# In units 17 to 30, VectorE sums the next unit's weight quarters behind the sum of two banks

## The chip, the core and the metric

The kernel runs on one core of a Trainium2 chip. The metric is the time of one launch on the device, in microseconds (us), as a median of several runs. A core has TensorE for matrix products (PE in the profile, PEld for its loading of weights), VectorE (DVE), ScalarE (ACT) and GpSimd (POOL) for work element by element, and SyncE (SP), whose queue here only starts transfers (DMA). Each engine takes its instructions in the order in which they are written and waits at semaphores for the others. TensorE writes into eight banks of 128 x 512 float32 numbers.

## What is computed

One transformer block of 2048 tokens and 512 features: a recurrent attention block on its first step, with a feed-forward half, and then a gated feed-forward block. The third stage, of which this case is, computes half of the last lines:

```
x = x + _L0_attn_ref(_layernorm(x), ...)
# _L0_ffn_ref, on h_shard = _layernorm(x):
gate_up = jnp.einsum('bsh,oh->bso', h_shard, w_gate_up)   # w_gate_up: 4096 x 512
gate, up = jnp.split(gate_up, 2, axis=-1)
h = jax.nn.silu(gate) * up
out = jnp.einsum('bsi,hi->bsh', h, w_down)
```

## The kernel before

**Three passes.** Every float32 product is made as three passes over numbers that are split in a high part (rounded by ScalarE) and a low part (what the rounding left, a subtraction on GpSimd or VectorE): high x high, high x low, low x high, summed in a bank.

**Units.** Both feed-forward parts are cut in 48 units. Units 0 to 15 (`is_key`) are the first part, two stages of eight; units 16 to 31 are the third stage, units 32 to 47 the fourth (`FIRST = (0, 8, 16, 32)`). A unit of the third stage takes 128 rows of gate and 128 of up against two blocks of 512 tokens. It does these four blocks of products with seven, in the manner of Strassen and Winograd: the four weight quarters and four sums of them (S1 to S4) meet seven combinations of the tokens (`combo`), which were made at the stage's start. The products land in four banks: X, Y, V and Z.

**TensorE's order in a unit** (`unit(u)` on TensorE) is: X product (p1), V product (p7), output tile, Y product (p6), X again (p2), output tile, Y (p5), output tile, Z (p4), Y (p3), output tile. A product is six matmuls, and so is an output tile, which multiplies the inner rows of an earlier unit with the matrix of the second layer. Unit 17 has two output tiles instead of four, behind p5 and p3.

**What VectorE does in a unit** (`unit(u)` on VectorE): it adds an output tile's bank to its rows (`accumulate`, L1664), makes Z from Y and the seventh product (`seed`, L1754), waits for p5, and makes V from the same two (`sum_v`, L1758), which the Y product p3 waits for, since it goes on in bank Y. Then it multiplies the Silu of X and of Y with Z and V (`gate`, L1768). Between these stand the sums of the next unit's weights (`sums(u + 1)`, L1603, L1604, L1606, L1608): from four quarters of 128 x 256 numbers it makes S1 to S4 in the tile `quart`.

**The weights' way.** SyncE loads the quarters of a unit into `quart` (`load_quart`, L510) when the unit before has no more use for it, that is when its low parts are done. ScalarE rounds the quarters (`unit_left_hi` part 0, L1113) and, when the sums are there, the four sums (part 1, L1116). GpSimd makes the low parts (`unit_left_lo`, L2072), two instructions for each part. TensorE's X product wants part 0, and its V product part 1. SyncE then keeps the whole in memory for the fourth stage (`keep_left`, L514).

**ScalarE's order in a unit**: copy of X (L1266), copy of V (L1272), rounding of the inner rows of the unit before (L1149), L1113, L1116, then the Silu of X (L1173), the rounding of the second layer's rows (L1126), and the Silu of Y (L1173). The X product of the next unit waits for the first Silu, its V product for both gates.

**GpSimd's order in a unit**: the low parts of the inner rows (L2112), L2072 twice for part 0, L2072 twice for part 1, the low part of the second layer's rows (L2107), and in some units two steps of the norm of a block (L2090, L2092).

**The norm of the second half of the tokens** runs beside the third stage. SyncE moves each of two blocks in 32 x 32 squares (`move_norm3`, L545, eight transfers behind `keep_left` of units 22 and 23 and of 27 and 28), stores rows of means and scales (L554), and loads them back broadcast (`load_rows`, L563). GpSimd (L2090, L2092) and for the last block VectorE too (L1720, L1722, at the end of units 28 and 29) wait for these rows. SyncE's queue is in order as well: `load_tall`, `load_quart`, `keep_left`, the moves and rows, unit by unit. `load_tall` (L525) brings rows of the second layer, L532 and L533 bring what the first part's end needs.

The order is written out by hand on every engine; nothing is scheduled by a program.

Of the kernel before, what the change touches and what calls it, by code (L numbers as in the profile page):

```python
# [78 lines left out]
FIRST = (0, KEY_UNITS, KEYS, KEYS + GATE_UNITS)  # L79
# [14 lines left out]
def made_place(stage, c):  # L94

    return (MADE_LATER if stage else MADE_FIRST).index(c)


def stage_of(u):
    return max(n for n in range(STAGE_COUNT) if FIRST[n] <= u)  # L100


def stage_start(u):
    return u in FIRST


def is_key(u):
    return u < KEYS
# [29 lines left out]
def tiles_in(u, slot):  # L138

    first, last = (tiles_until(u - 1), tiles_until(u)) if u else (0, 0)  # L140
    if u == KEYS + 1:
        return (first + slot - 2,) if slot >= 2 else ()
    if last == TILES:
        return tuple(range(first + slot, min(first + slot + 1, last)))
    share = (last - first) // 4
    return tuple(range(first + share * slot, first + share * (slot + 1)))
# [65 lines left out]
FRESH = tuple(u for u in range(UNITS) if stage_of(u) % 2 == 0)  # L212
# [6 lines left out]
def fresh_until(u):  # L219

    return len([f for f in FRESH if f < u])
# [34 lines left out]
def build(nc, x, x_feat, wts, wide, tall, down, vectors, identity, out):  # L256
# [3 lines left out]
    with ExitStack() as ctx:  # L260
# [1127 lines left out]
        def _(dve):  # L1388
# [210 lines left out]
            def sums(u):  # L1599

                done = 4 * fresh_until(u)
                dve.wait_ge(quart_loaded, 16 * (fresh_until(u) + 1))
                dve.tensor_tensor(quart[:, 4, :], quart[:, 0, :], quart[:, 3, :], ALU.add).then_inc(sums_done, 1)  # L1603
                dve.tensor_tensor(quart[:, 6, :], quart[:, 1, :], quart[:, 0, :], ALU.subtract).then_inc(sums_done, 1)  # L1604
                dve.wait_ge(sums_done, done + 1)
                dve.tensor_tensor(quart[:, 5, :], quart[:, 4, :], quart[:, 1, :], ALU.subtract).then_inc(sums_done, 1)  # L1606
                dve.wait_ge(sums_done, done + 3)
                dve.tensor_tensor(quart[:, 7, :], quart[:, 2, :], quart[:, 5, :], ALU.subtract).then_inc(sums_done, 1)  # L1608
# [20 lines left out]
            def first_chunk_right_lo():  # L1629
                for i in range(2):  # L1630
                    dve.wait_ge(right_hi, i + 1)
                    dve.tensor_tensor(right[:, 0, i, 1, :], tall_staged[i][:], right[:, 0, i, 0, :].bitcast(F32),
                                      ALU.subtract).then_inc(first_right_lo, 1)

            def combo_lo_of(stage, c):
                for k in range(2):
                    dve.wait_ge(combo_hi, 2 * (SEVEN * stage + made_place(stage, c)) + k + 1)
                    dve.tensor_tensor(combo[:, c, k, 1, :], combined(stage, c, k), combo[:, c, k, 0, :].bitcast(F32),  # L1638
                                      ALU.subtract).then_inc(combo_lo, 1)

            def make_t2(stage, tiles=range(2)):
                dve.wait_ge(combo_lo, 2 * (SEVEN * stage + made_place(stage, B11) + 1))
                dve.wait_ge(t_made, 8 * stage + 4)
                for k in tiles:
                    dve.tensor_tensor(combined(stage, T2, k), combined(stage, B22, k), combined(stage, T1, k),
                                      ALU.subtract).then_inc(t_made, 1)
# [8 lines left out]
            def accumulate(n):  # L1655
                h, s = divmod(n, SUBS)
                b = block_of_half(h)
                dve.wait_ge(out_psum, n + 1)
                tile = resid[:, b, s, :]
                if h // 2 in FIRST[:2]:  # L1660
                    dve.wait_ge(x1_kept[b], 16)
                    dve.tensor_copy(tile, A[s][:]).then_inc(added, 1)
                else:
                    dve.tensor_tensor(tile, A[s][:], tile, ALU.add).then_inc(added, 1)  # L1664
# [82 lines left out]
            def seed(u):  # L1747
                dve.wait_ge(p6, u + 1)
                dve.wait_ge(seventh_copied, u + 1)
                if u == 0:  # L1750
                    dve.wait_ge(sr_ready, SUBS * BLOCKS)
                elif is_key(u - 1):
                    dve.wait_ge(silu_done, silu_by(u - 1, 1))
                dve.tensor_tensor(Z[:], Y[:], seventh[:], ALU.add).then_inc(z_seeded, 1)  # L1754

            def sum_v(u):
                dve.wait_ge(p5, u + 1)
                dve.tensor_tensor(V[:], Y[:], seventh[:], ALU.add).then_inc(v_summed, 1)  # L1758
# [11 lines left out]
            def side_sum(kk, c):  # L1770

                dve.wait_ge(gated, 2 * (FIRST[3] + 2 * kk - KEYS) + (2 if c == T1 else 4))
                if c == T1:
                    if kk:
                        dve.wait_ge(side_lo, side_made(kk - 1, T2))
                    else:
                        dve.wait_ge(combo_lo, 2 * SEVEN * STAGE_COUNT)
                    dve.tensor_tensor(extra[:, 0, :], made[:, 1, :], made[:, 0, :], ALU.subtract).then_inc(side_sums, 1)
                elif c == T3:
                    dve.wait_ge(side_sums, 4 * kk + 1)  # L1780
                    dve.tensor_tensor(made[:, 1, :], made[:, 3, :], made[:, 1, :], ALU.subtract).then_inc(side_sums, 1)
                elif c == T2:
                    if kk:
                        dve.wait_ge(side_lo, side_made(kk - 1, T4))
                    dve.wait_ge(side_sums, 4 * kk + 1)
                    dve.tensor_tensor(extra[:, 1, :], made[:, 3, :], extra[:, 0, :], ALU.subtract).then_inc(side_sums, 1)
                else:
                    dve.wait_ge(side_lo, side_made(kk, B21))
                    dve.wait_ge(side_sums, 4 * kk + 3)
                    dve.tensor_tensor(made[:, 2, :], made[:, 2, :], extra[:, 1, :], ALU.subtract).then_inc(side_sums, 1)  # L1790
# [80 lines left out]
            def unit(u):  # L1871

                after = stage_of(u + 1) if u + 1 < UNITS and stage_start(u + 1) else None
                def some(slot):
                    for n in tiles_in(u, slot):
                        accumulate(n)

                if u == FIRST[3] + 1:
                    side_sum(0, T1)

                if after is not None:
                    combo_lo_of(after, B11)
                some(0)
                if after is not None:
                    make_t2(after, range(1))
                seed(u)
                if after is not None:
                    make_t2(after, range(1, 2))
                    combo_lo_of(after, T3)
                if u + 1 in FRESH and u > 1:  # L1890
                    sums(u + 1)
                if u == FIRST[2]:
                    dve.wait_ge(combo_lo, 2 * (SEVEN * 2 + made_place(2, T4) + 1))
                    combo_lo_of(2, B22)
                if stage_start(u) and u and u != FIRST[2]:
                    combo_lo_of(stage_of(u), T4)
                if is_key(u):
                    last_norm(u, 0)
                some(1)
                if u == 1:  # L1900
                    sums(u + 1)
                sum_v(u)
                if stage_start(u) and u and u != FIRST[2]:
                    combo_lo_of(stage_of(u), B22)
                if u == FIRST[3] + 1:
                    down_sums_of(0)
                if u == 0:
                    first_chunk_right_lo()
                if u in SUMS_UNIT and is_key(u):
                    right_sums(SUMS_UNIT.index(u))  # L1910
                if after is not None:
                    combo_lo_of(after, T2)
                    combo_lo_of(after, B21)
                some(2)
                if not is_key(u):
                    gate(u, 0)
                    gate(u, 1)
                if after is not None:
                    make_t4(after)
                some(3)  # L1920
                if after is not None and after != 2:
                    combo_lo_of(after, T1)
                last_norm(u, 1)
                if u in SUMS_UNIT and not is_key(u):
                    right_sums(SUMS_UNIT.index(u))
# [78 lines left out]
            for u in range(GROUP_UNIT):  # L2004
                unit(u)
# [290 lines left out]
```

## Time and profile before

| | us |
|---|---|
| median of 3 runs | 1047.43 |
| lowest and highest | 1046.34, 1048.19 |
| profiled execution | 1050.09 |
| its span, first to last instruction | 1048.3 |

The span is what the profile shows of the profiled execution, 1.8 us shorter than its time. TensorE is busy for 99% of it, VectorE 69%, GpSimd 60%, ScalarE 50%. A unit of the third stage takes 14.96 us where TensorE doesn't wait; unit 17 begins at 574.58 us and the V product of unit 31 at 788.09 us from the span's start. The times of instructions below are from that start. A matmul follows the one before it after 0.227 us, and its recorded end is modelled, so waits of TensorE are best read from the distance of starts.

### The profile page before, as it was taken

What the parts mean: (1) busy time and instruction counts of PE and PEld (TensorE: products, weight loads), DVE (VectorE), ACT (ScalarE), POOL (GpSimd) and SP (SyncE); (2) the same over time, 40 slices, a digit from 0 to 9 for tenths busy, and PEclk for the clock granted to TensorE, in tenths of its full rate; (3) what the DMA queues carried; (4) which work ended last, traced back from release to release, by engine and by line L of the source; (5) the groups of instructions that cost most, each with busy time, mean ns of one, the idle gap of its engine ahead of it and who ended that gap; (6) DMA issues with size and microseconds to landing.
All of it is one profiled execution on the core that took longest, in us unless ns stands there. A gap on an engine that the chain in (4) does not pass through costs nothing.

```text
span 1048.3 us, 13498 instructions
## 1 busy us (share of the span) xinstructions
PE 1035.7 (99%) x4616; PEld 855.3 (82%) x4616; DVE 719.6 (69%) x1227; ACT 520.4 (50%) x874; POOL 626.5 (60%) x512
## 2 busy tenths in 40 slices
PE   8999999999999999999999999989999999999999
PEld 7778888888888888888888788878878888888887
DVE  7899866786545565566569677688699566666655
ACT  6867888766444354333345433333335334444442
POOL 6796673735755555444547656579594356565652
PEclk9999999999999999999999999999999999999999
DMA  9100325277653344745634666765746445444532
GB/s 347 58 21 0 61 80 114 89 234 267 232 182 130 131 161 131 227 147 139 159 95 147 224 219 237 165 241 196 203 164 221 151 154 179 155 154 161 161 101 81
DMA packets 81123, 165.60 MB, mean 158 GB/s; under 512 B 39072, under 2 KB 39456, under 8 KB 76192
## 3 DMA queue, kind: packets, MB, share of 16 engines
q1 hardware_dynamic: 65600, 116.43, 33.5%
q0 software_dynamic: 15168, 48.24, 15.4%
q8 instruction: 37, 0.61, 0.2%
q14 instruction: 30, 0.25, 0.1%
q10 hardware_dynamic: 288, 0.09, 0.0%
HBM read 101.80 MB, written 58.74 MB: 153 GB/s over the span
## 4 chain that ended last, share of the span: by engine, by line
PE 78%; DVE 8%; POOL 5%; DMA 3%; SPq 2%; ACT 2%; issue 2%; DVEq 0%; ACTq 0%
PE bank L665 12%; PE bank L667 12%; PE bank L666 12%; PE bank L654 11%; PE bank L656 11%; PE bank L655 11%; POOL operand L2039 3%; PE bank L827 2%; PE bank L826 2%; PE bank L825 2%; SPq L545 2%; DMA quart<-wide 1%; DVE combo L1638 1%; POOL left L2072 1%; POOL weights L2027 1%
## 5 line engine op out<-in xcount | busy, mean ns | idle before, releaser
L665 PE MATMUL bank<-combo,left 128*128 128x512 f32 x672 | 262.1, 390 | 2.6 <-DVE bank L1758 2.6
L666 PE MATMUL bank<-combo,left 128*128 128x512 f32 x672 | 261.5, 389 | 0.0
L667 PE MATMUL bank<-combo,left 128*128 128x512 f32 x672 | 261.5, 389 | 0.0
L1664 DVE TENSOR_TENSOR resid<-bank,resid 128x512 f32<-128x512 f32 x176 | 119.9, 687 | 114.5 <-PE bank L656 113.6
L2112 POOL TENSOR_TENSOR inner<-made,inner 128x512 fp32r<-128x512 f32 x96 | 128.4, 1359 | 115.7 <-ACT inner L1149 115.6
L2072 POOL TENSOR_TENSOR left<-quart,left 128x512 fp32r<-128x512 f32 x96 | 115.9, 1230 | 78.1 <-ACT left L1116 39.4
L665 PEld LDWEIGHTS bank<-combo,left 128*128 128x128 f32 x672 | 126.1, 188 | 30.7 <-DVE bank L1758 4.3
L654 PE MATMUL bank<-right,inner 128*128 128x512 f32 x384 | 149.5, 389 | 1.6 <-POOL inner L2112 1.6
L656 PE MATMUL bank<-right,inner 128*128 128x512 f32 x384 | 149.4, 389 | 0.0
L655 PE MATMUL bank<-right,inner 128*128 128x512 f32 x384 | 149.4, 389 | 0.0
L666 PEld LDWEIGHTS bank<-combo,left 128*128 128x128 f32 x672 | 126.2, 188 | 26.1
L667 PEld LDWEIGHTS bank<-combo,left 128*128 128x128 f32 x672 | 126.2, 188 | 26.1
L2039 POOL TENSOR_TENSOR operand<-made,operand 128x512 fp32r<-128x512 f32 x64 | 83.3, 1354 | 32.7 <-ACT operand L993 32.7
L1158 ACT ACTIVATE made<-bank 128x512 f32<-128x512 f32 x64 | 37.6, 587 | 97.9 <-PE bank L667 97.9
L654 PEld LDWEIGHTS bank<-right,inner 128*128 128x128 f32 x384 | 72.1, 188 | 16.9 <-POOL inner L2112 2.0
L1768 DVE TENSOR_TENSOR made<-bank,made 128x512 f32<-128x512 f32 x64 | 44.1, 690 | 59.7 <-ACT made L1173 37.6
L1173 ACT ACTIVATE made<-bank 128x512 f32<-128x512 f32 x64 | 38.0, 593 | 94.4 <-PE bank L667 94.4
L655 PEld LDWEIGHTS bank<-right,inner 128*128 128x128 f32 x384 | 72.1, 188 | 15.0
L656 PEld LDWEIGHTS bank<-right,inner 128*128 128x128 f32 x384 | 72.1, 188 | 14.9
L1116 ACT ACTIVATE left<-quart 128x1024 fp32r<-128x1024 f32 x24 | 25.4, 1060 | 93.6 <-DVE quart L1608 93.6
L2107 POOL TENSOR_TENSOR right<-tall_staged,right 128x512 fp32r<-128x512 f32 x46 | 61.0, 1339 | 16.5 <-ACT right L1126 16.4
L654 PE MATMUL bank<-operand,weights 128*128 128x512 f32 x176 | 69.3, 394 | 1.1 <-DVE resid L1573 0.5
(199 smaller groups left out, 2018.1 us busy)
## 6 DMA issues: line engine op xcount, KB each, us to landing
kept_left<-left SPq DMA_DIRECT2D x24, 1792.0 KB, 8.1
left<-kept_left POOLq DMA_DIRECT2D x24, 1024.0 KB, 7.2
left<-kept_left POOLq DMA_DIRECT2D x24, 768.0 KB, 5.0
quart<-wide SPq DMA_DIRECT2D x24, 512.0 KB, 4.0
tall_staged<-tall SPq DMA_DIRECT2D x48, 256.0 KB, 5.2
raw<-kept SPq DMA_DIRECT2D x32, 256.0 KB, 5.4
landed<-wts SPq DMA_DIRECT2D x20, 256.0 KB, 6.3
resid<-x POOLq DMA_DIRECT2D x4, 1024.0 KB, 9.5
```

Source lines behind the costliest of these rows:

```text
L654: pe.matmul(acc, left(0), right(0), start=first, stop=False)
L655: pe.matmul(acc, left(0), right(1), start=False, stop=False)
L656: return pe.matmul(acc, left(1), right(0), start=False, stop=last)
L665: pe.matmul(acc[:], hi, combo[:, c, k, 0, :], start=fresh and k == 0, stop=False, skip_group_check=True)
L666: pe.matmul(acc[:], hi, combo[:, c, k, 1, :], start=False, stop=False, skip_group_check=True)
L667: mm = pe.matmul(acc[:], lo, combo[:, c, k, 0, :], start=False, stop=k == 1, skip_group_check=True)
L1664: dve.tensor_tensor(tile, A[s][:], tile, ALU.add).then_inc(added, 1)
L1768: dve.tensor_tensor(tile, (Z, V)[b][:], tile, ALU.mult).then_inc(gated, 1)
L2039: pool.tensor_tensor(place(kind, b, k, 1), made[:, (n + k) % RING, :], place(kind, b, k, 0).bitcast(F32), ALU.subtract).then_inc(op_lo, 1)
L2072: lo = pool.tensor_tensor(left[u % 2][:, 1, a[0]:a[0] + n, :], quart[:, a[0] + 1:a[0] + 1 + n, :], left[u % 2][:, 0, a[0]:a[0] + n, :].bit ...
L2107: pool.tensor_tensor(right[:, g % 2, i, 1, :], tall_staged[i][:], right[:, g % 2, i, 0, :].bitcast(F32), ALU.subtract).then_inc(right_lo, 1)
L2112: pool.tensor_tensor(inner[:, h % 4, i, 1, :], made_at(n), inner[:, h % 4, i, 0, :].bitcast(F32), ALU.subtract).then_inc(inner_lo, 1)
```

## The change

In the third stage, except for its first unit (16), `sums(u + 1)` moves from behind the seed to behind `sum_v`. That is so in 14 units, 17 to 30; unit 31 has no sums, since the fourth stage loads its weights ready made. Units of the first stage and units 15 and 16 keep their place.

```
@@ VectorE, unit(u) @@
                 if after is not None:
                     make_t2(after, range(1, 2))
                     combo_lo_of(after, T3)
-                if u + 1 in FRESH and u > 1:
+                if u + 1 in FRESH and u > 1 and u <= FIRST[2]:
                     sums(u + 1)
...
                 if u == 1:
                     sums(u + 1)
                 sum_v(u)
+                if u + 1 in FRESH and u > FIRST[2]:
+                    sums(u + 1)
                 if stage_start(u) and u and u != FIRST[2]:
                     combo_lo_of(stage_of(u), B22)
```

On VectorE, in unit 17: L1664 is the last accumulation of unit 16, L1754 the seed, L1603 to L1608 the sums (`quart`), L1758 is `sum_v`, and L1768 the two gates.

```order
 L1754 TENSOR_TENSOR bank<-bank,e_56 128x512
-L1603 TENSOR_TENSOR quart<-quart 128x256
-L1604 TENSOR_TENSOR quart<-quart 128x256
-L1606 TENSOR_TENSOR quart<-quart 128x256
-L1608 TENSOR_TENSOR quart<-quart 128x256
-L1758 TENSOR_TENSOR bank<-bank,e_56 128x512
+L1758 TENSOR_TENSOR bank<-bank,e_56 128x512
+L1603 TENSOR_TENSOR quart<-quart 128x256
+L1604 TENSOR_TENSOR quart<-quart 128x256
+L1606 TENSOR_TENSOR quart<-quart 128x256
+L1608 TENSOR_TENSOR quart<-quart 128x256
 L1664 TENSOR_TENSOR resid<-bank,resid 128x512
```

The sums are moved past `sum_v` alone. On VectorE in units 18 to 30, 24 and 29 among them, the accumulation of the output tile behind p2 (the first L1664) stands between seed and `sum_v` as well:

```order
-L1603 TENSOR_TENSOR quart<-quart 128x256
-L1604 TENSOR_TENSOR quart<-quart 128x256
-L1606 TENSOR_TENSOR quart<-quart 128x256
-L1608 TENSOR_TENSOR quart<-quart 128x256
-L1664 TENSOR_TENSOR resid<-bank,resid 128x512
-L1758 TENSOR_TENSOR bank<-bank,e_56 128x512
+L1664 TENSOR_TENSOR resid<-bank,resid 128x512
+L1758 TENSOR_TENSOR bank<-bank,e_56 128x512
+L1603 TENSOR_TENSOR quart<-quart 128x256
+L1604 TENSOR_TENSOR quart<-quart 128x256
+L1606 TENSOR_TENSOR quart<-quart 128x256
+L1608 TENSOR_TENSOR quart<-quart 128x256
```

The sums are moved past that accumulation and past `sum_v`. The other engines' orders are the same as before.

## Rows read from the trace of the kernel before

**Rows 1.** Head of the page: span, then busy time, share and count.

```profile
span 1048.3 us, 13498 instructions
...
PE 1035.7 (99%) x4616; PEld 855.3 (82%) x4616; DVE 719.6 (69%) x1227; ACT 520.4 (50%) x874; POOL 626.5 (60%) x512
```

**Rows 2.** Waits of TensorE from 500 to 830 us: total us, times, longest.

```profile
PE bank L665 <- DVE bank L1758: 2.6, 3, 1.3
```

**Rows 3.** Timeline of VectorE, unit 18: start, us, line, tiles.

```profile
593.49 0.70 DVE L1754 TENSOR_TENSOR bank<-bank,e 128x512 f32<-128x512 f32 x1 [0.67 <-PE bank L667]
594.10 0.69 DVE L1603 TENSOR_TENSOR quart<-quart 128x256 f32<-128x256 f32 x1
...
597.13 0.42 DVE L1608 TENSOR_TENSOR quart<-quart 128x256 f32<-128x256 f32 x1
...
598.08 0.69 DVE L1758 TENSOR_TENSOR bank<-bank,e 128x512 f32<-128x512 f32 x1
```

**Rows 4.** Timelines of ScalarE, GpSimd, SyncE's queue and TensorE, units 18 and 19.

```profile
597.60 1.06 ACT L1116 ACTIVATE left<-quart 128x1024 fp32r<-128x1024 f32 x1 [4.46 <-DVE quart L1608]
598.56 0.58 ACT L1173 ACTIVATE made<-bank 128x512 f32<-128x512 f32 x1
...
594.46 2.36 POOL L2072 TENSOR_TENSOR left<-quart,left 128x512 fp32r<-128x512 f32 x2
598.73 2.54 POOL L2072 TENSOR_TENSOR left<-quart,left 128x512 fp32r<-128x512 f32 x2 [1.92 <-ACT left L1116]
...
601.30 0.33 SPq L510 DMA_DIRECT2D quart<-wide  x1
...
602.81 0.39 PE L665 MATMUL bank<-combo,left 128*128 128x512 f32 x1
...
604.17 0.39 PE L665 MATMUL bank<-combo,left 128*128 128x512 f32 x1
```

**Rows 5.** Timeline of VectorE, unit 15: first and last of four sums.

```profile
551.00 0.41 DVE L1603 TENSOR_TENSOR quart<-quart 128x256 f32<-128x256 f32 x1
...
552.11 0.42 DVE L1608 TENSOR_TENSOR quart<-quart 128x256 f32<-128x256 f32 x1
```

**Rows 6.** Timelines of GpSimd and TensorE, unit 17.

```profile
581.42 2.17 POOL L2072 TENSOR_TENSOR left<-quart,left 128x512 fp32r<-128x512 f32 x2 [0.19 <-ACT left L1113]
...
582.74 0.39 PE L665 MATMUL bank<-combo,left 128*128 128x512 f32 x1
...
584.99 0.50 PE L665 MATMUL bank<-combo,left 128*128 128x512 f32 x1 [0.73 <-DVE bank L1758]
```

**Rows 7.** Timelines of SyncE's queue, VectorE, GpSimd and TensorE, units 23 and 24.

```profile
661.14 0.33 SPq L510 DMA_DIRECT2D quart<-wide  x1
...
673.67 0.38 SPq L554 DMA_DIRECT2D rows<-row_stats  x1
678.25 0.33 SPq L563 DMA_DIRECT2D extra<-rows  x1
...
690.55 1.40 DVE L1608 TENSOR_TENSOR quart<-quart 128x256 f32<-128x256 f32 x1
...
687.36 2.88 POOL L2112 TENSOR_TENSOR inner<-made,inner 128x512 fp32r<-128x512 f32 x2
...
688.85 0.50 PE L654 MATMUL bank<-right,inner 128*128 128x512 f32 x1 [1.56 <-POOL inner L2112]
...
693.21 0.50 PE L665 MATMUL bank<-combo,left 128*128 128x512 f32 x1 [1.33 <-DVE bank L1758]
```

**Rows 8.** Timelines of VectorE, GpSimd and TensorE, end of unit 28 and unit 29.

```profile
758.08 1.08 DVE L1720 TENSOR_TENSOR raw<-resid,extra 128x512 f32<-128x512 f32 x1 [1.29 <-DMA extra<-rows]
...
762.06 0.69 DVE L1754 TENSOR_TENSOR bank<-bank,e 128x512 f32<-128x512 f32 x1
...
766.15 1.40 DVE L1608 TENSOR_TENSOR quart<-quart 128x256 f32<-128x256 f32 x1
...
762.92 2.91 POOL L2112 TENSOR_TENSOR inner<-made,inner 128x512 fp32r<-128x512 f32 x2
...
768.81 0.50 PE L665 MATMUL bank<-combo,left 128*128 128x512 f32 x1 [0.51 <-DVE bank L1758]
```

More of the change, by code:

```diff
@@ L1889, in unit @@
                     combo_lo_of(after, T3)
-                if u + 1 in FRESH and u > 1:
+                if u + 1 in FRESH and u > 1 and u <= FIRST[2]:
                     sums(u + 1)
@@ L1902, in unit @@
                 sum_v(u)
+                if u + 1 in FRESH and u > FIRST[2]:
+                    sums(u + 1)
                 if stage_start(u) and u and u != FIRST[2]:
```

## The prediction

> **What bounds the kernel now.** I read the page's head first, then the waits of TensorE, then the timeline of one ordinary unit of the third stage engine by engine, and last the units in which TensorE waits. TensorE is busy for 99% of the span [rows 1], so whatever is not late for TensorE costs nothing: the question is only at which products it waits, by how much, and what will be late next. In and around the third stage it waits three times for the sum of two banks [rows 2], in units 17, 24 and 29, and once for the low part of an inner tile, in unit 24.
>
> An ordinary unit shows the frame. The X product and the V product of unit 19 start 1.36 us apart [rows 4], and every product and every output tile takes one such slot: the unit is 11 slots, 14.96 us. Counting back five slots from 602.81, the Y product that sum_v waits for (p5) starts at 596.01; counting back three more, the one that the seed waits for starts at 591.93, and the seed starts 1.56 us behind it [rows 3]. So sum_v could start at 596.01 + 1.56 = 597.57; it starts at 598.08 [rows 3]. Its result is wanted two slots before the end, at 600.09. In an ordinary unit the sums in front of it therefore cost nothing, and the change gains nothing there.
>
> **What the change moves.** In 14 units (17 to 30) the four sums go behind one accumulation and sum_v on VectorE. No instruction is added, and no DMA, wait or tile is. What queues behind the sums is the chain that makes the next unit's weights: ScalarE rounds four parts (L1116), with both Silus of the unit behind it in its queue, GpSimd makes the low parts (L2072), and SyncE then issues the load of the quarters of the unit after (L510) [rows 4].
>
> *The sums themselves, ordinary unit.* Before, they run from 594.10 to 597.55 [rows 3], 3.45 us, while GpSimd works on parts 0 to 2 from 594.46 to 596.82 [rows 4]. With GpSimd idle the four take from 551.00 to 552.53, 1.53 us [rows 5]. Behind sum_v, GpSimd is idle: its parts 0 to 2 are done at 596.82 and its next work needs the sums. I take the 1.53 us: start 597.57 + 0.60 (the spacing of sum_v's twin, the seed, and the first sum [rows 3]) = 598.17, end 599.70, against 597.55. The upper bound is the old 3.45 us, and I come back to it as a rival. In the slowed pieces a sum ends some 0.28 us behind the GpSimd instruction that runs beside it. The Trainium skill (SBUF — State Buffer, section "Who interferes with whom") says why: a VectorE instruction with two SBUF inputs and a GpSimd instruction exclude one another for a whole instruction. By that the sums take the lone time here, as rows 5 shows it; if both instead shared a rate, the old 3.45 us would stay, and the sum would be that of the third case below.
>
> *The chain behind them.* ScalarE's L1116 starts 2.15 us later, at 599.75; the Silu of X follows 0.96 us behind it [rows 4], at 600.71, and is wanted by the next X product at 602.81; GpSimd starts L2072 1.13 us behind L1116 [rows 4], at 600.88, and needs 2.54 us: 603.42. The V product wants it at 604.17 [rows 4]. So 0.7 us are left of 2.9 us, and the ordinary unit costs **0**. If that cover were gone, each us would be paid in every unit. The load of the next quarters goes out 2.15 us later too, at 603.4, but the sums that use it are later by as much, and it lands long before.
>
> *Unit 17, a gain.* The quarters land late here, ScalarE's first part (L1113) and GpSimd's parts 0 to 2 at 581.42 [rows 6] follow, the sums run beside these and sum_v behind them, and the product that wants V starts at 584.99, where the one before it began at 582.74 [rows 6]: 2.25 us instead of 1.36, so 0.89 us, and some 0.1 us that the first product behind a wait takes longer. After: p5 starts at 582.74 - 2 x 1.36 = 580.02, sum_v at 581.58, the sums at 582.2; GpSimd's parts 0 to 2 [rows 6] still overlap the first two, so they end at about 584.5, 0.2 us later than now. Then L1116 at 584.6 and L2072 until 584.6 + 1.13 + 2.54 = 588.3, while the V product of unit 18 would be free to start at 584.10 + 3 x 1.36 = 588.18. So about 0.15 of the 1.0 us comes back: **-0.86 us**.
>
> *Unit 24, a loss.* SyncE's queue holds, behind the load of quarters, the moves of the norm, the store and broadcast of its rows (L563 at 678.25) and the next load of quarters. It starts when unit 23's low parts are done, which is 2.15 - 0.86 = 1.29 us later than now, and between that load, at 661.14, and L563 it never waits for anything but its own transfers: eight moves, two loads, a store of rows and its landing. So the rows land 1.29 us later, GpSimd's norm rows and behind them the inner low parts (687.36) too, and the output tile at 688.85 that waits for them starts at 690.14 [rows 7]. From there the old wait for V goes: the product at 693.21 [rows 7] would start 1.36 us behind its predecessor, and 2 x 1.36 us or a little more behind the tile, at 692.99; 1.49 + 0.15 us are saved. The sums are again as slow as now (four of them beside GpSimd, the last at 690.55 for 1.40 us [rows 7]), 1.29 us later, so L1116 is at 693.3 and the low parts at 693.3 + 1.13 + 2.54 = 696.95, for a V product at 697.07: just in time. Net of unit 24: +2.15 - 1.64 = **+0.5 us**, to -0.35 in all.
>
> *Units 29 and 30, a loss.* The same queue, now for the fourth block: the rows land 1.95 us later than at 758.08 (2.15 and 0.15 for a GpSimd step that slides, less 0.35). VectorE itself waits for them ahead of the seed: L1720 at 760.03, the seed at 764.01 instead of 762.06 [rows 8]. The product behind it was due at 763.71, and starts at 764.75: one wait takes the place of the other, and the product that wants V starts three slots later at 768.8, as now (768.81 [rows 8]). Now sum_v runs early, at 766.3, but the sums stand at 766.9 with GpSimd's inner parts and parts 0 to 2 beside them (the first two now at 762.92 [rows 8], then at 764.9, and the next two until 769.75): they end near 770.5 instead of 766.15 + 1.40 = 767.55 [rows 8]. L1116 at 770.5, Silu of X 771.5 to 772.05, low parts 771.6 to 774.2. The next X product, due at 771.54, waits 0.5 us for the Silu, and V, due at 773.46 then, waits 0.8 us for the low parts: it starts at 774.24, where now it is at 773.03. Net of the pair: +1.21 - (-0.35) = **+1.55 us**. Unit 30's chain comes out at 789.2 for a V product due at 789.2: nothing more. Units 31 and later have no sums, and keep the shift.
>
> **Sum.** -0.86 + 0.5 + 1.55 = +1.2 us on the span of 1048.3 us [rows 1], so 1049.5; the profiled execution took 1050.09 us and the median of the runs is 1047.43, so I forecast **1048.6 us** for the median, a change of 0.1%. A measurement of this kernel tells about 0.2%, 2.1 us, from no change.
>
> **Rivals.**
>
> *Everything late falls, nothing comes back.* Then the three waits go: 1.0 + 1.6 + 0.8 = 3.4 us, and the time is 1044.0. For it: the waits are in the trace with VectorE's sum as their releaser [rows 2]. Against it: the later load and the later moves in SyncE's queue, and ScalarE's queue with the Silus behind L1116. It wants that queue to have slack, which it has not between 661 and 678 [rows 7]. 18%, with the mixed cases that gain over 2.1 us.
>
> *A late SyncE queue costs more than I reckon.* The same two places with larger sizes: the row transfers land on a DMA load that they did not meet before, or VectorE's norm row of unit 29, 1.08 us at 758.08 [rows 8], is caught behind a GpSimd instruction and takes as much longer as a sum does, 1.1 us. One us or two more at unit 30, paid by the X product through the Silu: +2.1 to +5 us, up to 1052.4. It decides from 0.9 us over my figures. 23%.
>
> *The margin of every unit is gone.* If the sums in their new place still take 3.45 us, L2072 ends at 605.3, 1.2 us behind the V product at 604.17, and in some 13 units that is +15 us: 1063. It begins to cost as soon as the four last over 1.53 + 0.7 = 2.2 us. Against it: nothing on GpSimd can run beside them. 7%.
>
> *It does nothing.* That the sums do move shows in the order of the two kernels; if waits for V are only swapped for waits on the Silu or the low parts, the time is that of before, 1047.4, inside my forecast.
>
> **How the numbers follow.** My case, within 2.1 us of before: 52%. Faster 18%, slower 23 + 7 = 30%. The range 1045.0 to 1052.2 leaves out the last rival (7%), the full form of the first (some 8%) and the edge of the second (3%).
>
> **What would show it right or wrong.** In the changed kernel's profile: ordinary units with sums of 0.41 us each and L1116 2.1 us later against sum_v's product; waits for the bank sum gone in the third stage; the wait for the inner tile in unit 24 longer by about 1.3 us; a wait of about 1 us for the seed in unit 29, and waits for the Silu and the weights' low parts at the start of unit 30. The forecast is wrong if TensorE waits in ordinary units (then the margin of 0.7 us was none), or if the output tile of unit 24 waits no longer than now (then SyncE's queue had slack).

## The result and the profile after

The changed kernel takes **1055.18 us** in the median of 6 runs (1052.87 to 1056.72), the kernel before 1048.01 us in 6 runs on the same chip (1046.34 to 1050.34). The ratio is 1.0056, with a 95% interval of 1.0045 to 1.0067: 5.9 us slower, outside the forecast range of 1045.0 to 1052.2. The medians themselves are 7.2 us apart, a little over the interval's end at 7.0; the account below is set against the ratio. The profiled execution's span grew from 1048.3 to 1053.5 us.

Where does the time go? The seed (L1754) comes once in each unit, so its start in both timelines dates the units. The changed trace is 0.76 us late from unit 0 to unit 17, ahead of anything that changed (in the other traces of this study that offset is -1.3 to +0.8 us); the last column takes it off.

| unit | seed before | seed after | shift since unit 17 |
|---|---|---|---|
| 17 | 578.86 | 579.62 | 0 |
| 18 | 593.49 | 593.76 | -0.49 |
| 25 | 702.04 | 702.61 | -0.19 |
| 28 | 746.58 | 747.10 | -0.24 |
| 29 | 762.06 | 765.49 | +2.67 |
| 30 | 777.85 | 780.66 | +2.05 |
| 31 | 792.87 | 799.13 | +5.50 |
| 32 | 807.33 | 812.60 | +4.51 |

From unit 32 on the shift stays as it is. So there is a gain of 0.5 us at unit 17, a small loss at unit 24, and two large losses: around unit 29, and in unit 31. TensorE's waits between 500 and 850 us (total us, times, longest) say what it waited for. They answer to [rows 2]:

```profile
PE bank L654 <- POOL inner L2114: 3.3, 1, 3.3
PE bank L665 <- DVE bank L1754: 3.2, 2, 1.7
PE bank L665 <- POOL left L2074: 0.6, 2, 0.4
PE bank L665 <- ACT made L1173: 0.3, 1, 0.3
```

The three waits for the sum of two banks (L1758) are gone, as the change would have it. In their place stand a longer wait for the inner tile, two waits for the seed (L1754), and small ones for the low parts and a Silu. (Lines behind 1902 are two higher than before: L2074 is L2072, L2114 is L2112.)

An ordinary unit of the timeline, unit 18, on VectorE, ScalarE, GpSimd and TensorE; it answers to [rows 3, 4]:

```profile
597.84 0.70 DVE L1758 TENSOR_TENSOR bank<-bank,e 128x512 f32<-128x512 f32 x1 [0.67 <-PE bank L667]
598.45 0.42 DVE L1603 TENSOR_TENSOR quart<-quart 128x256 f32<-128x256 f32 x1
...
599.57 0.43 DVE L1608 TENSOR_TENSOR quart<-quart 128x256 f32<-128x256 f32 x1
...
600.03 1.06 ACT L1116 ACTIVATE left<-quart 128x1024 fp32r<-128x1024 f32 x1 [5.74 <-DVE quart L1608]
...
601.17 2.55 POOL L2074 TENSOR_TENSOR left<-quart,left 128x512 fp32r<-128x512 f32 x2 [4.44 <-ACT left L1116]
...
604.44 0.39 PE L665 MATMUL bank<-combo,left 128*128 128x512 f32 x1
```

The four sums take 1.55 us from 598.45 to 600.00, since GpSimd is idle beside them. The low parts are done at 603.72, and the V product starts at 604.44, its slot: the margin is 0.7 us, and the unit costs nothing. Units 18 to 23 show no wait. This step of the prediction is right to a tenth of a us.

SyncE's queue, units 23 and 28, and what waits for it, against [rows 7, 8]:

```profile
663.59 0.33 SPq L510 DMA_DIRECT2D quart<-wide  x1
...
680.50 0.33 SPq L563 DMA_DIRECT2D extra<-rows  x1
...
743.17 10.68 SPq L545 DMA_DIRECT2D resid<-raw  x8
753.95 0.57 SPq L554 DMA_DIRECT2D rows<-row_stats  x1
756.44 0.33 SPq L563 DMA_DIRECT2D extra<-rows  x1
...
689.40 2.87 POOL L2114 TENSOR_TENSOR inner<-made,inner 128x512 fp32r<-128x512 f32 x2
...
690.90 0.50 PE L654 MATMUL bank<-right,inner 128*128 128x512 f32 x1 [3.33 <-POOL inner L2114]
...
761.54 1.08 DVE L1720 TENSOR_TENSOR raw<-resid,extra 128x512 f32<-128x512 f32 x1 [4.23 <-DMA extra<-rows]
...
765.49 0.68 DVE L1754 TENSOR_TENSOR bank<-bank,e 128x512 f32<-128x512 f32 x1
...
766.23 0.50 PE L665 MATMUL bank<-combo,left 128*128 128x512 f32 x1 [1.49 <-DVE bank L1754]
```

The output tile of unit 24 starts at 690.90 instead of 688.85: 2.05 us later, 1.29 us once the 0.76 us are off, the figure of the prediction. In unit 29 the rows come at 761.54 instead of 758.08.

The loss in unit 31, on VectorE and GpSimd, first after, then before:

```profile
791.10 2.30 DVE L1623 TENSOR_TENSOR extra<-raw 128x512 f32<-128x512 f32 x2
793.33 1.28 DVE L1626 TENSOR_TENSOR raw<-raw,raw 128x512 f32<-128x512 f32 x2
794.53 3.47 DVE L1638 TENSOR_TENSOR combo<-raw,combo 128x512 fp32r<-128x512 f32 x2
...
790.97 1.29 POOL L2109 TENSOR_TENSOR right<-tall_staged,right 128x512 fp32r<-128x512 f32 x1
...
793.95 3.50 POOL L2114 TENSOR_TENSOR inner<-made,inner 128x512 fp32r<-128x512 f32 x2 [0.26 <-ACT inner L1149]
...
799.87 0.50 PE L665 MATMUL bank<-combo,left 128*128 128x512 f32 x1 [1.70 <-DVE bank L1754]
```

```profile
787.54 1.29 DVE L1623 TENSOR_TENSOR extra<-raw 128x512 f32<-128x512 f32 x2
788.74 1.29 DVE L1626 TENSOR_TENSOR raw<-raw,raw 128x512 f32<-128x512 f32 x2
789.94 1.29 DVE L1638 TENSOR_TENSOR combo<-raw,combo 128x512 fp32r<-128x512 f32 x2
...
791.03 3.07 POOL L2112 TENSOR_TENSOR inner<-made,inner 128x512 fp32r<-128x512 f32 x2 [2.01 <-ACT inner L1149]
```

VectorE begins the fourth stage's token combinations at the end of unit 30 (L1623, L1626) and in unit 31 (L1638), ahead of the seed in its queue. Before, all six instructions were through at 791.2, and GpSimd's L2112 began at 791.03. After, GpSimd's L2109 and L2114 run beside them: L1623 takes 2.30 us instead of 1.29 and L1638 3.47 instead of 1.29, and the seed that stands behind is late for TensorE. Of the unit's 2.45 us, 2.0 are this wait, and 0.4 the V product's wait for unit 30's low parts (791.06).

### The profile page after: what moved, and what is told of

Its sections match the earlier page's. It is cut to its first block, busy times and chain, and to the rows that moved or that the text cites. A ratio compares the mean times of both kernels' runs of the same rounds, so it can differ in the third digit from the quotient of the medians.

```text
span 1053.5 us, 13498 instructions
## 1 busy us (share of the span) xinstructions
PE 1036.8 (98%) x4616; PEld 853.9 (81%) x4616; DVE 706.7 (67%) x1227; ACT 520.3 (49%) x874; POOL 622.8 (59%) x512
## 4 chain that ended last, share of the span: by engine, by line
PE 81%; DVE 5%; POOL 5%; ACT 2%; SPq 2%; issue 2%; DMA 2%; ACTq 0%; DVEq 0%; POOLq 0%
PE bank L665 13%; PE bank L667 13%; PE bank L666 13%; PE bank L654 11%; PE bank L656 11%; PE bank L655 11%; POOL operand L2041 2%; PE bank L826 2%; PE bank L827 2%; PE bank L825 2%; SPq L545 2%; DMA extra<-rows 1%; POOL left L2074 1%; POOL weights L2029 1%; PE bank L729 1%
## 5 line engine op out<-in xcount | busy, mean ns | idle before, releaser
L665 PE MATMUL bank<-combo,left 128*128 128x512 f32 x672 | 262.4, 391 | 4.3 <-DVE bank L1754 3.2
L667 PE MATMUL bank<-combo,left 128*128 128x512 f32 x672 | 261.5, 389 | 0.0
L1664 DVE TENSOR_TENSOR resid<-bank,resid 128x512 f32<-128x512 f32 x176 | 119.9, 686 | 128.8 <-PE bank L656 128.4
L2114 POOL TENSOR_TENSOR inner<-made,inner 128x512 fp32r<-128x512 f32 x96 | 126.8, 1342 | 101.8 <-ACT inner L1149 101.8
L2074 POOL TENSOR_TENSOR left<-quart,left 128x512 fp32r<-128x512 f32 x96 | 112.1, 1191 | 100.3 <-ACT left L1116 60.7
L665 PEld LDWEIGHTS bank<-combo,left 128*128 128x128 f32 x672 | 126.1, 188 | 33.7 <-DVE bank L1754 4.0
L654 PE MATMUL bank<-right,inner 128*128 128x512 f32 x384 | 149.5, 389 | 3.3 <-POOL inner L2114 3.3
L656 PE MATMUL bank<-right,inner 128*128 128x512 f32 x384 | 149.4, 389 | 0.0
L667 PEld LDWEIGHTS bank<-combo,left 128*128 128x128 f32 x672 | 126.1, 188 | 26.2
L654 PEld LDWEIGHTS bank<-right,inner 128*128 128x128 f32 x384 | 72.1, 188 | 18.6 <-POOL inner L2114 3.8
L656 PEld LDWEIGHTS bank<-right,inner 128*128 128x128 f32 x384 | 72.1, 188 | 15.0
L1768 DVE TENSOR_TENSOR made<-bank,made 128x512 f32<-128x512 f32 x64 | 44.1, 691 | 54.2 <-ACT made L1173 39.2
L2109 POOL TENSOR_TENSOR right<-tall_staged,right 128x512 fp32r<-128x512 f32 x46 | 61.6, 1352 | 18.8 <-ACT right L1126 18.8
L654 PE MATMUL bank<-operand,weights 128*128 128x512 f32 x176 | 69.6, 396 | 0.9 <-DVE resid L1573 0.5
```

What stands on the lines that cost most here:

```text
L654: pe.matmul(acc, left(0), right(0), start=first, stop=False)
L656: return pe.matmul(acc, left(1), right(0), start=False, stop=last)
L665: pe.matmul(acc[:], hi, combo[:, c, k, 0, :], start=fresh and k == 0, stop=False, skip_group_check=True)
L667: mm = pe.matmul(acc[:], lo, combo[:, c, k, 0, :], start=False, stop=k == 1, skip_group_check=True)
L1768: dve.tensor_tensor(tile, (Z, V)[b][:], tile, ALU.mult).then_inc(gated, 1)
L2074: lo = pool.tensor_tensor(left[u % 2][:, 1, a[0]:a[0] + n, :], quart[:, a[0] + 1:a[0] + 1 + n, :], left[u % 2][:, 0, a[0]:a[0] + n, :].bit ...
```

## The experiments

Two theories were set against each other. **The queue theory**: the loss comes at few places, through SyncE's queue (the moves and rows of the norm, units 24 and 29) and through GpSimd's later work in unit 31. **The margin theory**: each moved unit pays a little, since the low parts have only 0.7 us left. In the table, "profile" is the growth of the seed's shift from unit 17 to unit 32 against the trace of before, which leaves out what comes ahead of the change; "clock" counts the runs in which the mean granted clock was below 1.

| kernel | profile, us | ratio to before (95%) | clock below 1 |
|---|---|---|---|
| the change | +4.5 | 1.0056 (1.0045 to 1.0067) | 4 of 6 |
| e1, all but unit 30 | +3.8 | 1.0046 (1.0034 to 1.0059) | 5 of 5 |
| e2, moves first, sums as before | -3.0 | 0.9975 (0.9966 to 0.9983) | 0 of 11 |
| e3, moves first, the change | 0.0 | 1.0003 (0.9993 to 1.0013) | 0 of 11 |
| e4, unit 22 alone | +1.2 | 1.0027 (1.0017 to 1.0036) | 9 of 10 |
| e5, moves and rows first, sums as before | -4.4 | 0.9955 (0.9942 to 0.9969) | 0 of 5 |
| e6, e5 with unit 17 | -4.8 | 0.9956 (0.9944 to 0.9969) | 0 of 5 |
| e7, unit 30 alone | +0.4 | 1.0006 (0.9997 to 1.0014) | 0 of 12 |
| e8, unit 27 alone | +1.8 | 1.0019 (1.0009 to 1.0028) | 1 of 11 |
| e9, e5 with units 17 to 29 | -3.3 | 0.9976 (0.9967 to 0.9985) | 0 of 10 |
| e10, e5 with the whole change | -1.1 | 1.0002 (0.9993 to 1.0011) | 0 of 11 |

The kernel before was below full clock in 1 of the 68 runs that stood beside these.

### One unit at a time: e4, e8, e7

The sums go behind `sum_v` in the units of a tuple, everywhere else they stay:

```
+BEHIND = (22,)          # e8: (27,)   e7: (30,)   e1: tuple(range(17, 30))
...
-                if u + 1 in FRESH and u > 1:
+                if u + 1 in FRESH and u > 1 and u not in BEHIND:
                     sums(u + 1)
...
                 sum_v(u)
+                if u in BEHIND:
+                    sums(u + 1)
```

e4, unit 22:

> The kernel before, with the sums behind the sum of two banks in unit 22 alone. By the queue theory this one unit costs 2.15 us: unit 23's low parts are done 2.15 us later, so SyncE's moves start later, so the rows, and the output tile of unit 24 waits 3.8 us instead of 1.7: +2.1 us. By the margin theory it costs 0.3 us at most, and TensorE's wait in unit 24 stays as it was.

e8, unit 27:

> The kernel before, with the sums behind the sum of two banks in unit 27 alone, the twin of unit 22 in e4. By the queue theory the rows of the last block land 2.1 us later or more, VectorE's seed of unit 29 is late by as much, and since unit 29's sums stay ahead of its sum of two banks the wait there grows: +2.3 us. By the margin theory 0.3 us at most.

(In these traces L656 is L654 of before, L667 and L669 are L665 and L667, L1756 and L1760 the seed and the sum of two banks, L2116 is L2112.) One ordinary unit out of fourteen costs 1.0027, 2.8 us. TensorE doesn't wait in unit 22 or 23; it waits in unit 24, a unit in which nothing was moved. Waits of TensorE in e4 from 570 to 850 us:

```profile
PE bank L656 <- POOL inner L2116: 3.1, 1, 3.1
PE bank L667 <- DVE bank L1760: 2.3, 3, 1.3
```

The wait for the inner tile is 3.1 us where it was 1.56 [rows 7]; the waits for the sum of two banks are as before. In the profile that is +1.5 us at unit 24 (+1.2 by unit 32, as the waits of unit 29 came out smaller in this trace), less than the 2.15 expected: the load of quarters behind unit 22 went out 2.2 us later, but the moves and the landing of the rows took 0.7 us less. The rest of the 2.8 us is most likely the clock, below. e8 gives the same at the other place: +2.3 us at the seed of unit 29, the figure expected, and +1.8 by unit 32. The margin theory's 0.3 us is out for both.

e7, unit 30:

> The kernel before, with the sums behind the sum of two banks in unit 30 alone. What is tested is the loss in unit 31. If the later low parts of unit 30 alone make GpSimd collide with VectorE's first work for the fourth stage, the seed of unit 31 comes late: its slack is 1.3 us, the delay 1 to 3 us, so +1.0 us (0 to 1.7). If the loss needs the lateness that units 24 to 29 brought along, this kernel is the same as before.

From the seed of unit 30 to that of unit 32 the trace loses 0.95 us, which is the 1.0 expected; the two earlier waits came out smaller, so that +0.4 is left, and the ratio can't tell it from nothing. So unit 30's move alone makes unit 31's seed late, and by more when other lateness comes along (below). VectorE's first work for the fourth stage is slow in e7, and not in e1, where unit 30 isn't moved. First e7, then e1 (L1625 and L1640 are L1623 and L1638):

```profile
787.05 2.24 DVE L1625 TENSOR_TENSOR extra<-raw 128x512 f32<-128x512 f32 x2
790.41 2.38 DVE L1640 TENSOR_TENSOR combo<-raw,combo 128x512 fp32r<-128x512 f32 x2
```

```profile
791.62 1.28 DVE L1625 TENSOR_TENSOR extra<-raw 128x512 f32<-128x512 f32 x2
794.03 1.28 DVE L1640 TENSOR_TENSOR combo<-raw,combo 128x512 fp32r<-128x512 f32 x2
```

e1 leaves this one move out of the whole change:

> The change, but unit 30 keeps its sums where they were. Two theories. By the queue theory the loss comes at few places: SyncE's moves and norm rows that start later (units 24 and 29), and VectorE's first work for the fourth stage in unit 31, which GpSimd's later work of unit 30 runs into. Then this kernel loses the wait of 1.86 us for the seed of unit 31 and 0.4 us at its V product: +2.1 us against before in the profile from unit 17 on, where the change has +4.5. By the margin theory each of the 14 moved units pays about 0.3 us because the low parts are late for TensorE: +4.2 us, and unit 31's wait stays.

The wait in unit 31 is gone, and in its stead there is a wait of 0.8 us for the sum of two banks in unit 30, which neither the kernel before nor the change has. But the total fell only to +3.8 us, not to +2.1. Between the seeds of units 18 and 28 this trace loses 1.6 us where the change loses 0.25, and the reason is TensorE's clock, which fell after the wait in unit 24. The losses behind it are those of the change: +2.9 us at the seed of unit 29 in both. Against the change the ratio fell by 0.001, 1 us.

### The clock after a long wait: e1's trace

TensorE's timeline in e1 around the inner tile of unit 24, then the windows (us, busy time and count of each engine, PEclk, DMA share, GB/s):

```profile
686.31 0.39 PE L669 MATMUL bank<-combo,left 128*128 128x512 f32 x1
689.95 0.61 PE L656 MATMUL bank<-right,inner 128*128 128x512 f32 x1 [3.26 <-POOL inner L2116]
690.36 0.63 PE L657 MATMUL bank<-right,inner 128*128 128x512 f32 x1
...
692.92 0.63 PE L668 MATMUL bank<-combo,left 128*128 128x512 f32 x1
693.35 0.51 PE L669 MATMUL bank<-combo,left 128*128 128x512 f32 x1
693.70 0.39 PE L667 MATMUL bank<-combo,left 128*128 128x512 f32 x1
```

```profile
670.00:686.00 16.00, 16.00 (x72) 13.27 (x71) 10.32 (x16) 4.77 (x8) 5.12 (x5) 1.00 0.76 154
...
690.00:694.00 4.00, 4.00 (x11) 3.14 (x12) 3.58 (x4) 0.95 (x1) 3.61 (x3) 0.57 0.81 214
694.00:700.00 6.00, 6.00 (x28) 4.99 (x27) 4.04 (x5) 2.30 (x5) 5.81 (x4) 1.00 0.34 95
```

After 3.4 us without a matmul the next eight come 0.41 to 0.43 us apart and the ninth 0.35, instead of 0.227, and the granted clock of that stretch is 0.57 in the mean: most of it at the lower level of 1.2 GHz. Ten starts, from 689.95 to 693.70, take 3.75 us instead of 9 x 0.227 = 2.04: the fall costs **1.7 us** on top of the wait. (In the changed kernel's trace, where the clock stayed, the same ten starts behind the wait take 2.17 us, 690.90 to 693.07; against that it is 1.6.)

The fall came in 5 of 5 runs of e1 and in 9 of 10 of e4, which wait 3.1 to 3.4 us in unit 24, in 4 of 6 of the changed kernel, whose profiled run was one without it, and in 2 of the 144 runs of all the others, before included, whose traces show 2.0 us at most in one piece in the third stage. So it is the likely missing part of e4: 1.2 in a trace with full clock, 2.8 in the ratio. Run by run that isn't shown: e4's one run at full clock took 1051.65 us, the nine others 1052.26 in the mean.

The Trainium skill (TensorE: Matmul & The Clock Gate, section "Part 1: The HAM clock gate") says that an idle array loses its clock and gets it back with work. e1's trace agrees (0.57 behind the wait, 1.00 from 694 us on); in the changed kernel's trace a wait as long, 3.33 us, did not bring the clock down.

### SyncE's queue: e2 and e3

In units 23 and 28 the second half of the moves goes ahead of the two transfers that wait for GpSimd's low parts; e2 has the sums as before, e3 has the whole change:

```
+                for j in range(PAIRS, BLOCKS):
+                    if u == MOVE_UNIT[j] + 1:
+                        move_norm3(j, range(SQUARES // 2, SQUARES))
                 if u + 1 in FRESH:
                     load_quart(u + 1)
                 if u in FRESH:
                     keep_left(u)
                 for j in range(PAIRS, BLOCKS):
                     if u == MOVE_UNIT[j]:
                         move_norm3(j, range(SQUARES // 2))
-                    if u == MOVE_UNIT[j] + 1:
-                        move_norm3(j, range(SQUARES // 2, SQUARES))
```

> The kernel before, with one edit in SyncE's queue: in units 23 and 28 the second half of the norm's moves stands ahead of the load of quarters and of the store of the weights, which wait for GpSimd's low parts. The sums stay in their old place. By the queue theory the moves start some 4 us earlier, the rows are there early, and the waits of units 24 and 29 go: 1.7 + 1.6 + 0.8 = 4.1 us faster, -0.4%. By the margin theory nothing changes: 0.

> The changed kernel, with the same edit in SyncE's queue as e2. By the queue theory units 24, 29 and 30 no longer wait, the 0.5 us of unit 17 stay gained, and only unit 31's wait of some 2 us stays: -0.5 - 3.4 - 0.8 + 2.0 = -2.6 us against before. By the margin theory it stays at +4 to +5 us.

e2 is faster than before, by 0.25%: a place of the queue in which nothing was changed by this case's diff bounded the kernel already. TensorE's waits in unit 24 fell from 3.4 us to 0.4, but the wait in unit 29 stayed (1.1 us in this trace, 0.8 before), so -3.0 instead of -4.1. SyncE's queue in e2 shows why:

```profile
656.76 5.58 SPq L545 DMA_DIRECT2D resid<-raw  x8
662.43 0.57 SPq L510 DMA_DIRECT2D quart<-wide  x1
663.04 1.42 SPq L514 DMA_DIRECT2D kept_left<-left  x1
...
666.30 1.21 SPq L554 DMA_DIRECT2D rows<-row_stats  x1
674.30 0.33 SPq L563 DMA_DIRECT2D extra<-rows  x1
```

The eight moves are issued in 5.6 us instead of some 10, but the store of rows, now close behind the store of weights (1.8 MB), takes 8.0 us to land instead of 4.6 [rows 7], and L563 waits for it. e3 came out at 0.0, not at -2.6: unit 31 costs +2.5 us (expected 2.0), and in unit 24 there are still waits for the inner tile (0.7), the Silu (0.4) and the low parts (0.7): the rows reach GpSimd only at 683.10, and its norm rows, inner parts and parts 0 to 2 then run until 691.1, beside the moved sums, which take 4.2 us (687.65 to 691.83). But the same edit takes 4.5 us off the changed kernel and 3.0 off the old one; the margin theory expected nothing from it in either.

### Rows ahead of the weights: e5, e6, e9, e10

```
                     if u == MOVE_UNIT[j] + 1:
                         move_norm3(j, range(SQUARES // 2, SQUARES))
+                        keep_rows(j)
                 if u + 1 in FRESH:
                     load_quart(u + 1)
...
                 for j in range(PAIRS, BLOCKS):
                     if u == ROWS_UNIT[j]:
-                        keep_rows(j)
                         load_rows(j)
```

> The kernel before, with SyncE's moves as in e2 and the store of the norm's rows (L554) directly behind them, ahead of the load of quarters and the store of the weights. In e2 that store, queued behind 1.8 MB of weights, took 8 and 9.3 us to land and held SyncE's queue all that time. By the queue theory it now lands in some 4 us, so the rows are there 4 us earlier than in e2, and the wait for the sum of two banks in unit 29 goes as well: -4.1 us against before in the profile, where e2 has -3.0. If the landing time doesn't come from the weights ahead of it, it stays at -3.0.

SyncE's queue in e5:

```profile
657.16 5.58 SPq L545 DMA_DIRECT2D resid<-raw  x8
662.85 0.57 SPq L554 DMA_DIRECT2D rows<-row_stats  x1
663.52 1.38 SPq L510 DMA_DIRECT2D quart<-wide  x1
...
667.50 0.70 SPq L563 DMA_DIRECT2D extra<-rows  x1
```

The store lands within 4.7 us, the broadcast goes out 10.7 us earlier than before (678.25 [rows 7]; 9.7 with the offset of this trace taken off), and from unit 18 on TensorE waits for nothing until the fourth stage. All that is left of [rows 2] is unit 17. e5 is **1044.61 us against 1049.40**, ratio 0.9955: with e6 the best kernel of this study, and with the sums in their old place.

e6 adds the change in unit 17 alone:

> As e5, and the change of this case in unit 17 alone, the unit where it gained 0.5 to 0.8 us in the changed kernel and in e1: -4.1 - 0.6 = -4.7 us. By the margin theory the moved unit costs a little instead.

-4.8 us in the profile, -0.4 against e5, and the same ratio. Over the six traces with unit 17 moved, the seed of unit 18 comes 0.43 to 0.85 us sooner. So the one unit in which the change does good is below what can be measured. The whole change on e5's queue, first without unit 30 and then with it:

> SyncE's queue as in e5, and the sums behind the sum of two banks in units 17 to 29. If the queue carried all of the loss of units 24 to 30, the moved units now cost nothing: e5's -4.4 us less the 0.5 us of unit 17, about -4.8 us against before in the profile, TensorE's clock full in every run. By the margin theory it is 3 us slower than e5.

> As e9, with unit 30 too, so the whole change on top of e5's queue. What it adds to e9 is unit 31's late seed alone: +1.0 us as in e7 where the lateness is only its own, up to +2.3 us as in e3; so -3.8 to -2.5 us against before. By the margin theory it is only 0.3 us slower than e9.

Here the queue theory missed. e9 is at -3.3 us, 1.1 us behind e5, not 0.4 ahead. The low parts miss the V product by 0.5 us in unit 24 and 0.3 in unit 30. Both times GpSimd's parts 0 to 2 come late and stand beside the first two moved sums, which take 0.97 and 0.96 us in unit 23, 0.74 and 0.96 in unit 29, instead of 0.42: in unit 23 since the quarters were issued behind the moves and landed at 669.6, in unit 29 since GpSimd had its norm rows and inner parts to do until 760.6. And unit 30, whose sums stay in front, has the wait of 0.8 us for the sum of two banks that e1 has. That is the margin theory in small: it holds in the two units where something else took the 0.7 us. e10 adds unit 30 and loses 2.3 us more, the upper end of what was expected; the trace shows unit 31's wait again, 1.97 us at the same product. (0.6 of the 2.3 us arise at unit 29, where the two programs are still the same, so two traces differ by as much without a cause in the code.) So this loss doesn't need late rows; with the moved units before it, it is 2.4 to 2.5 us from the seed of unit 30 to that of unit 32 (e3, e10, the change), and alone 0.95 (e7). Against the same kernel with unit 30 left alone (e9, e1), which pays 0.7 to 0.8 us in unit 30, moving it costs 1.7 us.

## Why the prediction was wrong

*Ordinary units cost nothing*: right, in each figure. *Unit 17 gains 0.86 us*: half right, 0.49 us in this trace (0.43 to 0.85 in the six that have it). The sums ended 0.3 us later than reckoned, and the V product of unit 18 waited 0.4 us for the low parts (589.35 instead of 588.94) and ran 0.1 us longer; I had put both at 0.15.

*Unit 24 loses 0.5 us, by SyncE's queue*: right. The tile came 1.29 us later as worked out, the wait for V went, and the net was +0.3 us. That the figure is met to the digit is luck: the queue started 1.69 us later (663.59 against 661.14 [rows 7], 0.76 off), since unit 17 had given back less, the store of rows took 4.31 us instead of 4.58, and 0.2 us more came back on the way to the tile. e4 and e2 show the cause from both sides.

*Units 29 and 30 lose 1.55 us*: right in mechanism, too small in size. To unit 30's seed it was +2.3 us (-0.24 to +2.05). The term that was mis-sized is the rows' delay, put at 1.95 us: it was 3.46 - 0.76 = 2.7 us. The load ahead of the moves went out 2.05 us later, much as reckoned; the eight moves then took 10.68 us of the queue instead of 9.40, which I had carried over unchanged; the store of rows took 0.84 us less, the broadcast 0.2 more. The seed of unit 29 was late by as much, 0.7 us over the forecast, and so was all behind it. The moves were not a fixed length. Behind unit 27 they took 5.3 us in e2, 9.4 to 9.5 in the kernel before, e4 and e7, where unit 27 isn't moved, and 10.4 to 11.0 in e8, e1 and here, where it is. The waits that follow at the start of unit 30 came near the forecast: 0.46 us for the Silu (0.5) and 0.7 for the low parts (0.8).

*"Units 31 and later have no sums, and keep the shift"*: this step failed, and it is the largest part of the miss. Unit 31 has no sums, but its first combinations stand on VectorE behind unit 30's gates and beside GpSimd's low parts, and the slack of its seed was 1.3 us. I had followed GpSimd's chain into unit 31 only as far as the V product, and there too it came 0.4 us late where I had it just in time. It costs +2.45 us (5.50 at the seed, 4.51 in unit 32, against 2.05). The same rule that I used for the sums, that VectorE and GpSimd wait out each other's whole instructions, gives it: two L1638 beside L2114 take 3.47 us instead of 1.29.

*The clock* was in no step. I priced waits of TensorE at their length; a wait of 3.3 us can cost 1.7 us more. Counted once in each of 4 of 6 runs, an estimate from e1's trace, that is 1.1 us of the mean, and with the profile's +4.5 us it comes to 5.6, within the interval of the measured 5.9 (4.7 to 7.0). It is a low estimate: the mean granted clock of the four is 0.998, 0.997, 0.997 and 0.996, and e1's profiled run, with one fall, has 0.998. No trace shows what more fell in three of them.

The sum again, with what was measured: -0.5, +0.3, +2.3, +2.4 (unit 31), +1.1 (clock), 5.6 us in all, against a forecast of 1.2. Of the rivals, "a late SyncE queue costs more than I reckon" was the one that came true, for 0.7 us of rows that came later than reckoned, a sixth of the miss; its range to +5 us was too narrow because it knew neither unit 31 nor the clock. What stays open: why the same eight moves hold SyncE's queue for 9.4 us or 10.7 by whether unit 27 is moved, and why the clock fell in every run of e1 and not in every run of the change, with the same wait.

## What to carry to other kernels

When a step is moved in an engine's queue, follow the chain behind it until it meets the next irregular place, and not just to the next product: 2.15 us more in the ordinary units were free, and were paid at two transfers in a queue of another engine and at one change of stage. A transfer that waits for slow work should not stand in a queue ahead of transfers that are ready: putting eight moves and a small store ahead of it was worth 4.7 us, five to ten times what the change gains in its best unit. Keep a wait of TensorE short even where it looks cheap.

## What the runs showed of the hardware

In kernels with a wait of 3.1 to 3.5 us in one piece TensorE's granted clock fell in 18 of 21 runs, in e1's trace for eight matmuls of 0.41 to 0.43 us; in those whose trace shows 2.0 us at most in the third stage, in 2 of 144. It doesn't show in every trace of the same kernel, so a profiled execution at full clock can leave out a loss of the other runs, 1.7 us by e1's trace.

A small store (4 KB of rows) took 8.0 and 9.3 us to land in e2 when it was issued within 4 us behind 1.8 MB of weights on the same queue, and 4.7 and 3.3 us in e5 ahead of them; in the kernel before, 10 to 12 us behind them, 4.6 and 3.3. The Trainium skill (DMA: Bandwidth & Descriptors, section "Two DMAs through the same engine are not ordered") says that within one queue of one DMA engine descriptors start in order. The two placements agree with that, but no run shows which transfer the store waited for.

An instruction of VectorE with two inputs in SBUF is longer beside one of GpSimd: two 128x512 of L1638 took 1.29 us with GpSimd idle, 2.38 (e7) and 3.47 us (the change, e3) beside its inner low parts.
